# A transformer block in one launch: the value products moved between the second row scores and the second column scores, and the tasks moved to the ends of slots

## The reference

```python
sa, ca, ga, sb, cb, gb = (_silu(c) @ wmod) in six parts; ga, gb kept at 0.25 or more in size
h = _layernorm(x) * (1 + ca) + sa
q, k, v = split(h @ w_qkv); 16 heads of 8
attn = softmax(q @ k.T / sqrt(128)) @ v
x = x + ga * (attn @ w_out)
h = _layernorm(x) * (1 + cb) + sb
x = x + gb * moe(h)
# moe: softmax router over 8 experts, the best 2 weighed to sum 1,
# out = sum_e weight_e * (silu(h @ w_gate[e]) * (h @ w_up[e])) @ w_down[e], hidden size 176
```

## Time and profile before

| what | value |
|---|---|
| median of 3 runs | 710.53 us |
| lowest and highest | 709.41 and 711.87 us |
| profiled execution | 714.01 us |
| its span, first to last instruction | 712.2 us |
| mean granted TensorE clock in it | 0.933 |
| busy: PE, DVE, ACT, POOL | 629.3, 536.1, 453.9, 267.2 us |

### The profile page before, as it was taken

The page is one execution under the profiler, slowest core; times in us unless marked ns, Lnnn a source line. Parts: engine busy times, 40 slices in busy tenths (PEclk is TensorE's granted clock), DMA queues, the critical chain, the costliest instruction groups (busy, mean ns, idle before and its releaser), DMA issues.

```text
span 712.2 us, 12638 instructions
## 1 busy us (share of the span) xinstructions
PE 629.3 (88%) x3413; PEld 285.4 (40%) x3413; DVE 536.1 (75%) x809; ACT 453.9 (64%) x859; POOL 267.2 (38%) x384
## 2 busy tenths in 40 slices
PE   4159889899989999998999988989889999999995
PEld 3111223323322322322332331322667777777773
DVE  3696788888886877876868878800888888888885
ACT  2107878778767768777768778767455555555553
POOL 3521021221221222122122131351557777777773
PEclk9657999999999989999989999966999999999998
DMA  7703405205203303401600600124334444444411
GB/s 179 202 12 91 162 3 126 87 19 118 95 18 90 121 17 78 134 17 33 178 16 12 200 17 5 43 92 117 115 106 137 136 156 122 133 153 138 136 40 30
DMA packets 48971, 65.58 MB, mean 92 GB/s; under 512 B 9432, under 2 KB 30432, under 8 KB 48928
## 3 DMA queue, kind: packets, MB, share of 16 engines
q1 hardware_dynamic: 46304, 64.32, 31.1%
q10 hardware_dynamic: 2624, 0.79, 0.5%
HBM read 47.26 MB, written 17.83 MB: 91 GB/s over the span
## 4 chain that ended last, share of the span: by engine, by line
PE 42%; issue 17%; POOL 16%; ACT 11%; DVE 7%; DMA 4%; ACTq 1%; SPq 1%; POOLq 0%; DVEq 0%
PE o_acc L1182 16%; POOL hid_lo L599 13%; PE ring L1172 10%; ACT probs L643 9%; PE s_row L1137 6%; DVE negmax L851 3%; DMA max_scr<-negmax_T 2%; PE ring L1101 1%; PE ring L1085 1%; DVE probs L1029 1%; PE ring L1117 1%; POOL h_lo L605 1%; SPq L312 1%; PE ring L1090 1%; PE ring L1087 1%
## 5 line engine op out<-in xcount | busy, mean ns | idle before, releaser
L851 DVE TENSOR_REDUCE negmax<-s_row 128x2 f32<-128x1024 f32 x256 | 306.7, 1220 | 80.1 <-PE s_row L1137 77.0
L643 ACT ACTIVATE probs<-ring 128x512 f32<-128x512 f32 x512 | 272.4, 599 | 89.2 <-PE ring L1172 80.7
L1172 PE MATMUL ring<-q_stack,k_stack 64*128 64x512 bf16 x512 | 148.7, 406 | 31.6 <-ACT probs L643 22.9
L599 POOL TENSOR_TENSOR hid_lo<-probs,hid_hi 128x512 fp32r<-128x512 f32 x87 | 128.5, 1493 | 63.7 <-ACT hid_hi L787 63.7
L1182 PE MATMUL o_acc<-probs,v_aug 128*32 128x512 f32 x1024 | 146.3, 645 | 0.0
L1137 PE MATMUL s_row<-k_stack,q_stack 64*128 64x512 bf16 x512 | 106.2, 412 | 20.3 <-DMA k_stack<-k_scr 12.2
L787 ACT ACTIVATE hid_hi<-probs 128x512 fp32r<-128x512 f32 x88 | 55.6, 632 | 85.0 <-DVE probs L1029 84.9
L1172 PEld LDWEIGHTS ring<-q_stack,k_stack 64*128 64x128 bf16 x512 | 38.1, 96 | 114.7 <-ACT probs L643 91.9
L1137 PEld LDWEIGHTS s_row<-k_stack,q_stack 64*128 64x128 bf16 x512 | 25.1, 95 | 139.0 <-DVE negmax L851 66.2
L1029 DVE TENSOR_TENSOR probs<-probs,q_stack 128x512 f32<-128x512 f32 x56 | 62.4, 1114 | 15.8 <-POOL hid_lo L599 13.7
L507 POOL CAST negmax_parts<-negmax 128x16 bf16<-128x16 f32 x32 | 6.3, 197 | 167.0 <-DVE negmax L851 167.0
(11 more groups left out here) (134 smaller groups left out, 703.4 us busy)
## 6 DMA issues: line engine op xcount, KB each, us to landing
q_scr<-q_parts SPq DMA_DIRECT2D x48, 128.0 KB, 2.4
k_scr<-k_parts SPq DMA_DIRECT2D x48, 128.0 KB, 2.4
q_stack<-q_scr SPq DMA_DIRECT2D x8, 768.0 KB, 6.4
k_stack<-k_scr SPq DMA_DIRECT2D x8, 768.0 KB, 8.1
q_stack<-combT_scr SPq DMA_DIRECT2D x24, 256.0 KB, 3.4
k_stack<-combT_scr SPq DMA_DIRECT2D x16, 224.0 KB, 2.9
q_stack<-combT_scr SPq DMA_DIRECT2D x16, 192.0 KB, 2.8
q_stack<-combT_scr SPq DMA_DIRECT2D x16, 160.0 KB, 2.5
```

The source lines that it names most:

```text
L599: nc.gpsimd.tensor_tensor(hid_lo[k % HIDDEN][:], weighed[(par + k) % 2], hid_hi[k % HIDDEN][:], ALU.subtract).then_inc(s["hid_split"], 1)
L643: nc.scalar.activation(probs[t % 2][:, j, :], ring[PLACE[u] % RING][:], ACT.Exp, scale=INV_SCALE).then_inc(s["exp_done"], 1)
L851: nc.vector.tensor_reduce(negmax[n % 2][:, 2 * half:2 * half + 2, qc], s_row[pair % 2][:], AX.X, ALU.max, negate=True).then_inc(s["row_max ...
L1172: nc.tensor.matmul(ring[PLACE[u] % RING][:], k_stack[par][at:at + KS, head // 2, P * kc:P * (kc + 1)], q_stack[par][at:at + KS, head // 2, ...
```

## The change

The four value products of a slot stood behind its last column score, or behind a task at (t, 1). Now they stand between the second pair of row scores and column scores 2 and 3. All tasks that stood at (t, 0) stand at the end of a slot, at (t, 1), or at (t, 2) if there are two; both are now behind column scores 2 and 3, one after the other. attnT moves to slot 6 and proj to slot 7; the others keep their slot. The rest of q moves from place (1, 1) to (2, 0), that of k from (2, 1) to (3, 0), the middle parts from (2, 0) and (3, 0) to (2, 1) and (3, 1). The five steps of the statistics start at (8, 0) in place of (6, 1), two to a half slot, and the aggregate stands at (9, 0) in place of (8, 1). The router's exponential and VectorE's steps behind it come half a slot later. What each instruction computes is the same, and so are their numbers.

```diff
     TASKS = {
-        (0, 0): "xT", (0, 2): "max1", (1, 0): "q", (2, 0): "k", (3, 0): "o0", (3, 2): "o1", (4, 0): "o2", (4, 2): "max2",
-        (5, 0): "o3", (5, 1): "attnT", (6, 0): "proj", (8, 1): "max3", (9, 0): "v", (10, 2): "x1T", (11, 1): "router",
-        (12, 1): "max0", (15, 0): "combT",
+        (0, 1): "xT", (0, 2): "max1", (1, 2): "q", (2, 2): "k", (3, 1): "o0", (3, 2): "o1", (4, 1): "o2", (4, 2): "max2",
+        (5, 1): "o3", (6, 1): "attnT", (7, 1): "proj", (8, 2): "max3", (9, 2): "v", (10, 2): "x1T", (11, 2): "router",
+        (12, 1): "max0", (15, 2): "combT",
     }
...
             ORDER += [G * t + 2 * half, G * t + 2 * half + 1]
-            if (t, half) in TASKS:
-                ORDER.append(TASKS[t, half])
-        if (t, 2) in TASKS:
-            ORDER.append(TASKS[t, 2])
+        for step in (1, 2):
+            if (t, step) in TASKS:
+                ORDER.append(TASKS[t, step])
...
-            MIDDLE_Q, MIDDLE_K, ROUTER_EXP, FIRST_BLOCK = (2, 0), (3, 0), (12, 0), (14, 1)
+            MIDDLE_Q, MIDDLE_K, ROUTER_EXP, FIRST_BLOCK = (2, 1), (3, 1), (12, 1), (14, 1)
...
-            REST = {(1, 1): "q", (2, 1): "k"}
-            LN2_STATS = [(6, 1), (7, 0), (7, 1), (8, 0), (8, 1)]
-            ROUTE = {(12, 1): softmax_sum, (13, 0): sort, (13, 1): pick, (14, 0): denominator}
+            REST = {(2, 0): "q", (3, 0): "k"}
+            LN2_STATS = {(8, 0): (0, 1), (8, 1): (2, 3), (9, 0): (4,)}
+            ROUTE = {(12, 2): softmax_sum, (13, 1): sort, (14, 0): pick, (14, 1): denominator}
...
-                            if at in LN2_STATS:
-                                ln2_stats(b - 1, LN2_STATS.index(at))
+                            for step in LN2_STATS.get(at, ()):
+                                ln2_stats(b - 1, step)
...
                             row_scores(b + 1, 1 - par, t + AHEAD - SLOTS, half)
+                        if half == 1 and t > 0:
+                            weigh(b, par, t - 1)
+                        elif half == 1 and not first:
+                            weigh(b - 1, 1 - par, SLOTS - 1)
                         for j in range(2 * half, 2 * half + 2):
                             col_scores(b, par, t, j, first, last)
-                        turn((t, half))
-                    if t > 0:
-                        weigh(b, par, t - 1)
-                    elif not first:
-                        weigh(b - 1, 1 - par, SLOTS - 1)
+                    turn((t, 1))
                     turn((t, 2))
```

## The result

The changed kernel takes 699.6 us (median; 698.9 to 700.3) against 710.4 us (709.4 to 711.9) of the kernel before in the same comparison: a ratio of 0.985, interval 0.982 to 0.987, 10.8 us less. The forecast was 711.3 with 703.5 as the low end of its range, so it missed. The profiled execution took 698.9 us with a span of 697.1, against 714.0 and 712.2 before. The profiled execution before is a slow one of its kernel (granted clock 0.933, 3.6 us above the median of 710.4), so the two traces lie 15.1 us apart where the medians lie 10.8 apart.

A forecast was written before the change was run, and what follows sets the result against it. A loop through TensorE and ScalarE, 2.68 us per plain slot, was taken as the bound, no engine being full. Middle bodies +0.8, first body +1.1 and last -1.2 gave +0.7 us on the median: 711.3 us, range 703.5 to 718.5.

The forecast's parts named there:

- the Sum: Adds the slots by body: middle bodies 53.55 against 53.42 (+0.8 for six), first body +1.1, last -1.2, total +0.7 us.
- I take no difference: Last body's later part at half clock: same time before and after; whole last body -1.2 us, ends -3 and +1.5.
- (a) to (f): Walk through a middle body's slots: plain 2.67 us, behind a task 3.17 or more, behind q and k 3.69, slot 15 2.94.
- rival 1: Slower: clock falls in every middle body behind the stalled x1T, +4 to +6 us, 716.5 us; chance 0.20.
- Rival 2: Slower: V's wait costs 0.05 to 0.1 in each of some 110 slots, +6 to +11, 719 us; chance 0.12.
- The branch back costs both the same: At a loop's end, the branch back was taken to cost both orders the same, no difference.
- (e): Second layer norm, middle bodies: x1n comes late, TensorE stands 1.5 us ahead of x1T, slot 11 takes 4.19 us.
- The first part: First body ahead of slots 4 to 15: V no longer queues behind a half-clock q product, estimated -1.3 us.
- Rival 3: Faster: x1T doesn't wait, slot 11 is 3.17 in place of 4.19, 6.1 us less, 705 us; chance 0.22.

The follow-up runs named there:

- wide products at the router: Kernel before with four unused column-score-shaped products ahead of the router's products in the middle bodies; 716.5 us, ratio 1.017.
- the second trace of after: The changed kernel run once more, unchanged, for a further trace; 702.2 us in one execution.
- V alone: Kernel before with only the value products moved between the second row scores and column scores 2 and 3, tasks as they were; 715.6 us, ratio 1.009.
- router twice: The changed kernel with the router's products issued two times; 705.4 us, ratio 0.998 to the kernel before.
- router moved: Kernel before with the router's products behind the value products of slot 11 in place of ahead of them; 705.2 us, ratio 0.997.

## Why the prediction was wrong

711.3 us was forecast and 699.6 measured. The step that failed is in the Sum: the time at half clock was taken to be the same in both orders. For the middle bodies one quiet body stood for all six (+0.8 forecast, -9.1 between the traces), and for the last body's part at half clock it says "I take no difference" (-1.2 forecast, -7.1 between the traces). The runs showed 15 to 19 us at half clock after the first 60 where before has 56 to 59. Why the new order has less of it stays open. The walk through the slots was right.

**Right: the walk through the slots, (a) to (f).** Plain slot 2.61 (2.67 forecast), behind a task 3.09 (3.16), slot 1 behind xT and max1 3.94 (3.94), the slot of the stall 4.09 (4.19), slot 15 2.81 (2.94). Slots 2 to 5, behind q, k, o0 with o1, and o2 with max2, took 3.13, 3.77, 4.04 and 3.49 where 3.69, 3.69, 3.48 and 3.29 were forecast: c2 now stands behind V, so that its wait for q_rest (166.25) falls into the slot after; the four come to 14.43 against 14.15. A quiet middle body is 53.25 where 53.55 was forecast. The walk rested on timelines of before alone. (Two small slips: the total of +0.7 gives 711.2 and not 711.3, and rivals 1 and 2 with a fifth of the forecast are 0.41 and not 0.39.)

**Right: no price for V's wait.** V starts 0.53 behind c1, and slots behind a task take 3.09, less than the 3.16 without a price. Rival 2 is excluded.

**Wrong: the Sum, in its term for the middle bodies.** It took the difference to the stretch from 156.01 to 209.43, six times. That body was the quickest of before's six. The six together took 332.64, 55.4 each. The new order's bodies came out near their quickest (53.9 each), the old order's did not. The right base was the mean of the bodies, and then the question what becomes of the 2.0 us by which it stands above the best: falls behind the router 4.9 in all, loop's branch 1.8, ScalarE's wait for the store 1.5. "The branch back costs both the same" was off by 1.8 in before's disfavour between these two traces; in the further ones the branch costs the new order 1.2 to 1.4 more. (e) did not ask what ScalarE's wait in slot 6 becomes.

**Wrong: the last body.** -1.2 was forecast with -3 as its end, and it was -7.1. The step that failed is "I take no difference" for the part at half clock: before stays in it to 494, after leaves it at 474. But the same order of work left it early as well, without a change in that body (50.7 us, wide products at the router). So part of the -7.1 is the traced execution of before, and how much the order decides is not shown.

**The first part: -2.9 against -1.3, in part chance.** Up to V(3) the second trace of after takes 65.67 us, so that V ahead of the q product gives 1.0 there and 2.9 in the first. In before, q took 2.07 at half clock with V queued behind it; in after, the clock rises during V and q takes 1.12:

```profile
55.94 2.07 PE L1085 MATMUL ring<-hT,wqk_sb 128*128 128x512 f32 x2
```

```profile
56.53 1.48 PE L1181 MATMUL o_acc<-probs,v_aug 128*32 128x512 f32 x8
...
58.26 1.12 PE L1084 MATMUL ring<-hT,wqk_sb 128*128 128x512 f32 x2
```

**The clock and rival 1: wrong sign.** The prediction let the clock fall more often or as often as before, never less often; that half of the cases was missing among the rivals. This is the step that cost the forecast most: by the estimate above some 9 of the 10.8 us. The clock came out higher (0.99 for 0.96 in the middle bodies), though TensorE is less busy (290.6 of 323.6 us against 308.0 of 332.6). The rule of the Trainium skill (TensorE: Matmul & The Clock Gate, Part 4: PE-mode transpose), that transposes count less as a busy TensorE, spoke for falls behind x1T. The trace of after, with the same transposes behind a 1.4 us stall and no fall, does not bear that out as a price.

**Rival 3 was right in its price.** x1T did wait. With the wait taken out, a body is 1.18 shorter, where rival 3 had 1.02. That x1T would not wait in the changed kernel, as rival 3 had it, did not happen: the time under 705 came for another reason than the one given to it.

**Still open.** Why the new order keeps the clock up. Shown is that V alone and the changed kernel have fewer us at half clock than before (medians of 54 and, for the router twice, 49, against 78 and 76 beside them), that neither the router ahead of V nor a shortage of wide products beside it nor a larger share of narrow ones brings the falls, and that none came behind a 1.4 us stall where six came behind one of 4.5 us. V's place can't be the whole account: with V at the end behind a task there were no falls either. In the last body no run tells apart the order and the moment at which the body begins: in the old order it took 56.7, 56.5, 56.5, 51.1 (router moved) and 50.7 (nothing moved in it).

## What to carry over

A forecast by one quiet body must ask what the other bodies lose above it, and whether the change keeps that loss; take the mean of the bodies as the base and list the excess by place. Where a profile shows stretches at half clock, their ends belong among the rivals on both sides, since an order that leaves the amount of work as it is can win or lose more by them than by its own slots (here some 11 of the 15 us between the two traces: 4.9 behind the router and 6 in the last body). Two moves that both cost time alone can pay together: V ahead of a waiting c2 fills that wait, V behind it adds to it. And one trace is one execution: its span and mean clock, held against those of the other executions, tell whether its half-clock time is the usual one.

## What the runs showed of the hardware

- The granted clock did not follow TensorE's busy share: 93% busy before with a clock of 0.96 in the middle bodies (308.0 of 332.6 us), 90% busy after with 0.99 (290.6 of 323.6).
- A stall of 1.4 us ahead of transposes never lowered the clock (none of 24 bodies), one of 4.5 us did in six of six, for 3.5 to 7 us each.
- At 1.2 GHz the old order's last body stayed there for 27 us and in another run, with nothing changed in that body, for only 7 us (wide products at the router). In the last 18.5 of the 27 us TensorE was busy 94% of the time (17.38 us), and the clock did not rise:

```profile
475.90:494.40 18.50, 17.38 (x64) 4.12 (x62) 1.97 (x17) 11.30 (x24) 4.98 (x9) 0.50 0.50 143
```

- A value product that waits for an exponential costs no more than its steps: V started 0.52 to 0.54 behind c1 in 46 slots of after, where 0.53 was counted from slots without such a wait.
- Executions of one kernel differ in their time at half clock by 40 us (53 to 94 us in 39 of before), and each of these us goes with about 0.26 us of span (an estimate, from the line above).
